# An expert layer in high and low parts: three quarters of the second weights split, one quarter plain

## The chip, the cores and the metric

One core of a Trainium2 chip runs the whole kernel. The metric is the time of one execution in microseconds (us), the median of several runs; less is better. Engines: TensorE (PE) multiplies, VectorE (DVE), ScalarE (ACT) and GpSimd (POOL) do the elementwise work, SyncE (SP) issues DMAs.

## The reference

Two layers over x, 32 sequences of 128 tokens with 256 features. The first is a cross attention with 16 heads, which is not touched here. The second sends each of the 4096 tokens to one of 8 experts, the one with the largest product with its centroid, and computes with that expert's weights

```python
xn = xhat[None, :, :] * ln_g[:, None, :] + ln_b[:, None, :]
h = jax.nn.relu(jnp.einsum('etd,efd->etf', xn, w1) + b1[:, None, :])
y = x[None, :, :] + jnp.einsum('etf,edf->etd', h, w2) + b2[:, None, :]
```

followed by a gate between y and x. Here d is 256 and f is 1024. All inputs and outputs are float32. The second product, h times w2, is what the change is about.

## The kernel before, in words

The attention stage writes each token's row, sorted by expert, to memory. The expert stage reads them back in blocks of 256 tokens of one expert. There are up to 23 blocks, and those that turn out empty are skipped at run time; blocks below n_early (6) are placed by an early table, those from 6 on by a late table that is made once all tokens are counted (late_blocks on DVE).

A float32 product on TensorE is made in one of two ways. Plain: the operands stay float32, and each product shows as two instructions. In parts: each operand is split into a high part (a copy rounded to fp32r) and a low part (the operand less its high part), and three products are summed, high with high, low with high, high with low (PASSES). Block 0 is plain altogether. From block 1 on, layer_1 (L902) is in parts, and layer_2 (layer_2_split) is in parts for the first FS of the FC = 8 chunks of the hidden width, by in_parts (L932), and plain for the other chunks, by plain (L938). Both are done for each of the two halves of 128 tokens. Before, FS is 4.

Who makes what, for block s:

- TensorE runs layer_1(s+1), then layer_2_split(s), and so on. layer_1 is made in four pairs of chunks, each into a bank of PSUM of its own, which it may write again when ReLU of the block before has read it. It waits for split_xn(s) and low_weights_1(s) as well; layer_2_split waits for all parts of the second weights and of the hidden values.
- ACT, in the order of its queue: normalise_rows(s+2) (L1186), high_weights_1(s+2) (L1170, 2048 columns), relu_parts(s+1) (L1241, four pairs), row_gain_bias(s+2) (L1208, writes c_in), high_weights_2(s+1) (L1251, the first FS chunks of w2, 256 columns each). ReLU writes the chunks that are to be split into hid_raw (y_t in the profile), the others into hid_plain (prob_t).
- DVE: low_weights_1(s+2) (L1635), split_hidden(s+1) (a cast L1644 and a subtraction L1645 for each pair of chunks), split_xn(s+2) (L1629, L1631), transpose_rows(s+3) (L1620), finish(s) (L1658 reads PSUM, L1663 writes the result rows, once for each half). Between blocks 1 and 3 it also chooses the last experts (L1509 to L1515) and makes the late table (L1561 to L1614).
- POOL: add_base(s+2) (L1891), low_weights_2(s+1) (L1898, the first FS chunks of w2), write_rows(s) (L1903, an indirect DMA for each half).
- SP loads rows, weights, vectors and biases. The first weights of blocks 6 and on are loaded once the late table is there.

Each engine works its queue in order; semaphores hold an instruction back, and what stands behind it. In split_hidden a pair of chunks is cast and subtracted, and f_hl counts it. hid_hi and hid_lo have two copies, for even and odd blocks. hid_raw has two places of 512 columns, one for each pair of a block with FS = 4.

Of the kernel before, what the change touches and what calls it, by code (L numbers as in the profile page):

```python
# [10 lines left out]
ALU = mybir.AluOpType  # L11
AXIS_X = mybir.AxisListType.X

P = 128
# [6 lines left out]
BLOCK = 2 * P  # L21
# [15 lines left out]
FIRST_SPLIT = 1  # L37
# [71 lines left out]
def build(nc, x, x_t, ctx_in, ln_pack, w_q, w_kv, w_out, w_out_t, centroids_t, consts, experts, b2, out):  # L109
# [7 lines left out]
    FC = d_ff // P  # L117
# [19 lines left out]
    with ExitStack() as top:  # L137
        def sem(name):
            return top.enter_context(nc.semaphore(name))

        def sbuf(scope, name, shape, dtype=F32):
            return scope.enter_context(nc.sbuf_tensor(name, shape, dtype))
# [23 lines left out]
        with ExitStack() as a:  # L166
# [14 lines left out]
                r_more = sbuf(late, "r_more", [P, NBLOCK - NR, 2, ROW])  # L181
            q_s = [sbuf(a, f"q_{h}", [P, 2, 2, 2 * P], F32R) for h in ("hi", "lo")]
            k_s = [sbuf(a, f"k_{h}", [P, 2, 2, BANK], F32R) for h in ("hi", "lo")]
            FS = FC // 2
            with ExitStack() as late:
                hid_hi = sbuf(late, "hid_hi", [P, 2, FS, BLOCK], F32R)
                sbuf(late, "hid_between", [P, 3 * FS * BLOCK])
                hid_lo = sbuf(late, "hid_lo", [P, 2, FS, BLOCK], F32R)
            v_n = sbuf(a, "v_n", [P, 2, 2, 2, BANK])
            y_t = sbuf(a, "y_t", [P, KC, 2, 2 * P])  # L190
            prob = sbuf(a, "prob", [P, 2, 4, 2, 2, 2, Q])
            prob_t_even = sbuf(a, "prob_t", [P, 2, 4, 2, 2, 2, Q])
# [98 lines left out]
            f_hl = sem("f_hl")  # L291
# [14 lines left out]
            def w1_raw(s):  # L306

                if s == 1:
# [9 lines left out]
            hid = v_n[:, 0].rearrange("p a b n -> p (a b n)").rearrange("p (f t) -> p f t", f=FC)  # L318
            hid_hl = (hid_hi, hid_lo)
            hid_raw = y_t[:].rearrange("p c b t -> p c (b t)")  # L320
            hid_plain = prob_t_even[:].rearrange("p b a h i s q -> p b (a h i s q)").rearrange("p s (f t) -> p s f t", f=FC - FS)
            w2_hl = [[w[:].rearrange(rule)[:, 0:FS * d_model].rearrange("p (f d) -> p f d", f=FS) for w in pair] for pair, rule in
                     ((head_out, "p b c t -> p (b c t)"), (w_o, "p c n -> p (c n)"))]
            blocks = "p (j h i s k) -> p j h i s k"
# [8 lines left out]
            raw = [w.rearrange("p (c n) -> p c n", c=KC) for w in  # L333
                   (w1_ring[:, 0], w1_ring[:, 1], r_ring[:].rearrange("p n i c -> p (n i c)")[:, 0:KC * inner])]
# [44 lines left out]
            def wait_made(eng, item):  # L379

                if item[0] == "ft":
                    eng.wait_ge(f_t, item[1] + 1)
                elif item[0] == "fy":
                    eng.wait_ge(f_y, 2 * item[1] + item[2] + 1)
                else:
                    eng.wait_ge(s_job, made_before[item] + 1)
# [70 lines left out]
            def wait_low(eng, g, side):  # L457
                if g == 0:
                    eng.wait_ge(s_lo_first[side], 1)
                else:  # L460
                    eng.wait_ge(s_lo, 2 * (g - 1) + side + 1)
# [211 lines left out]
            def _(pe):  # L673
# [245 lines left out]
                def layer_2_split(s):  # L919
# [4 lines left out]
                    def wait_parts(s):  # L924
                        pe.wait_ge(f_w2h, s - FIRST_SPLIT + 1)
                        pe.wait_ge(f_w2l, s - FIRST_SPLIT + 1)
                        pe.wait_ge(f_hl, FS // 2 * (s - FIRST_SPLIT + 1))

# [121 lines left out]
            def _(act):  # L1050
# [175 lines left out]
                def relu_parts(s):  # L1226

                    b1 = vec_ring[:, s % NR, 2 * KC:]
                    if s == FIRST_SPLIT:
                        wait_low(act, n_pairs - 1, 1)  # L1230
                        wait_made(act, ("pv", n_steps - 1))
                    for i in range(FC // 2):
                        act.wait_ge(f_h, FC // 2 * (s - 1) + i + 1)
                        if i < FS // 2 and s > FIRST_SPLIT:
                            act.wait_ge(f_hl, FS // 2 * (s - 1 - FIRST_SPLIT) + i + 1)
                        elif i == FS // 2 and s >= 2:
                            wait_made(act, ("fy", s - 2, 1))
                        for f in (2 * i, 2 * i + 1):
                            at = slice((f % 2) * BLOCK, (f % 2 + 1) * BLOCK)
                            dst = hid_raw[:, i, at] if f < FS else hid_plain[:, s % 2, f - FS, :]  # L1240
                            ins = act.activation(dst, psum[:, i, at], ACT.Relu, bias=b1[:, f:f + 1])  # L1241
                        ins.then_inc(f_ha, 1)

# [84 lines left out]
                high_outputs(n_steps - 1)  # L1328
                high_weights_1(2)
                relu_parts(1)  # L1330
                row_gain_bias(2)
                normalise_rows(3)
                high_weights_1(3)
                high_weights_2(1)
                relu_parts(2)
                row_gain_bias(3)
                gate_of(n_batches - 2)
                gate_of(n_batches - 1)
                normalise_rows(4)
                high_weights_1(4)  # L1340
                high_weights_2(2)
                relu_parts(3)
                row_gain_bias(4)
                high_weights_2(3)
# [14 lines left out]
            def _(dve):  # L1359
                chained = [0]  # L1360

                def then_next(ins):

                    chained[0] += 1
                    ins.then_inc(s_dve, 1)
                    dve.wait_ge(s_dve, chained[0])
# [271 lines left out]
                def split_hidden(s):  # L1638
                    for i in range(FS // 2):
                        dve.wait_ge(f_ha, FC // 2 * (s - 1) + i + 1)  # L1640
                        if i == 0:
                            wait_made(dve, ("fy", s - 2, 1) if s > FIRST_SPLIT else ("pv", n_steps - 1))
                        hi, lo = [h[:, s % 2, 2 * i:2 * i + 2, :].rearrange("p f t -> p (f t)") for h in hid_hl]
                        then_next(dve.tensor_copy(hi, hid_raw[:, i, :]))  # L1644
                        dve.tensor_tensor(lo, hid_raw[:, i, :], hi, ALU.subtract).then_inc(f_hl, 1)  # L1645

                def finish(s):
                    dve.wait_ge(f_b[s % NR], 16 * (s // NR + 1))
# [123 lines left out]
                places(n_batches - 3)  # L1772
                low_weights_1(2)
                split_hidden(1)
                new_rows(n_batches - 2)
                split_xn(2)
                new_rows(n_batches - 1)
                choose(n_batches - 2)
                choose(n_batches - 1)
                low_weights_1(3)  # L1780
                split_hidden(2)
                split_xn(3)
                finish(1)
                read_ranks(n_pairs - 1)
                places(n_batches - 2)
                places(n_batches - 1)
                low_weights_1(4)
                split_hidden(3)
                split_xn(4)
                late_blocks()  # L1790
# [240 lines left out]
```

## Time and profile before

| | |
|---|---|
| three runs, median | 1053.16 us (1052.61 to 1053.6) |
| the profiled execution | 1052.73 us |
| its span, first to last instruction | 1050.9 us |
| granted TensorE clock | 0.999 of full speed |
| busy: TensorE, DVE, ACT, POOL | 99%, 80%, 66%, 54% |
| DMA, mean rate | 181 GB/s |

The span is what the profile shows; its times run from the span's start. A line L938 is line 938 of the kernel. "out<-in" names tiles, and since tiles share memory, a hidden value can carry the name of an attention tile: y_t is hid_raw, prob_t is hid_plain, w_o_hi and head_out_hi are the high second weights of odd and even blocks, k_hi and k_lo the parts of the block's input, x_in the result rows.

### The profile page before, as it was taken

How to read it: one execution, taken by the hardware profiler on the slowest of the kernel's cores; microseconds unless marked ns; L12 is line 12 of the kernel's file. 1: busy time of each engine (PE TensorE's matmuls, PEld its weight loads, DVE VectorE, ACT ScalarE, POOL GpSimd, SP SyncE). 2: the span in 40 equal slices, each digit the busy share in tenths (PEclk: the TensorE clock that was granted, in tenths of full speed). 3: DMA queues.
4: the chain of work that ended last, by engine and by line, in shares of the span. 5: the costliest groups of instructions: out<-in, count | busy, mean ns of one | idle time of the engine just before them, and what ended most of it. 6: DMA issues, size and time to landing. Idle time of an engine off the chain costs nothing.

```text
span 1050.9 us, 24670 instructions
## 1 busy us (share of the span) xinstructions
PE 1041.6 (99%) x8610; PEld 940.5 (89%) x8610; DVE 844.9 (80%) x1979; ACT 688.7 (66%) x1838; POOL 565.3 (54%) x665
## 2 busy tenths in 40 slices
PE   9999999999999999999999999999999999999997
PEld 7889898988888888889898989889888999999997
DVE  7878888878888888888888879888887797767663
ACT  6765757675666767666757575766566666676761
POOL 1744464646454555545464646465444667566663
PEclk9999999999999999999999999999999999999999
DMA  6665657585757576767667585856356868777760
GB/s 212 160 169 148 170 156 189 146 215 142 201 146 197 142 193 155 200 156 197 159 168 185 142 210 137 213 144 171 91 153 196 307 198 294 250 234 234 249 194 31
DMA packets 159666, 190.57 MB, mean 181 GB/s; under 512 B 17454, under 2 KB 149038, under 8 KB 154673
## 3 DMA queue, kind: packets, MB, share of 16 engines
q1 hardware_dynamic: 155088, 179.09, 62.4%
q0 software_dynamic: 3360, 8.53, 2.2%
q8 instruction: 72, 1.18, 0.4%
q10 hardware_dynamic: 1088, 1.31, 0.4%
q14 instruction: 58, 0.47, 0.1%
HBM read 65.72 MB, written 46.07 MB: 106 GB/s over the span
## 4 chain that ended last, share of the span: by engine, by line
PE 96%; DVE 2%; POOL 1%; ACT 1%; DMA 0%; issue 0%; POOLq 0%; DVEq 0%
PE psum L742 17%; PE psum L775 16%; PE psum L812 11%; PE psum L902 10%; PE psum L791 10%; PE psum L827 9%; PE psum L761 8%; PE psum L938 6%; PE psum L932 5%; PE psum L830 1%; PE psum L883 1%; PE psum L914 1%; DVE neg_max L1410 1%; DMA c_in<-in_ctx_in 0%; PE psum L856 0%; DVE w_lo L1545 0%
## 5 line engine op out<-in xcount | busy, mean ns | idle before, releaser
L1823 POOL TENSOR_TENSOR prob<-prob,inv_sum 128x512 f32<-128x512 f32 x172 | 177.7, 1047 | 190.1 <-DVE inv_sum L1416 189.2
L1133 ACT ACTIVATE prob<-psum,neg_max 128x256 f32<-128x256 f32 x344 | 160.2, 478 | 38.8 <-DVE neg_max L1410 38.5
L1410 DVE TENSOR_REDUCE neg_max<-psum 128x2 f32<-128x512 f32 x256 | 161.9, 672 | 27.7 <-PE psum L791 27.5
L1422 DVE STREAM_TRANSPOSE prob<-prob 128x512 f32<-128x512 f32 x172 | 118.5, 698 | 12.3 <-POOL prob L1823 11.9
L1823 POOL TENSOR_TENSOR w_ring<-w_ring,inv_sum 128x512 f32<-128x512 f32 x76 | 78.1, 1041 | 76.0 <-DVE inv_sum L1416 75.7
L1140 ACT ACTIVATE head_out_hi<-psum 128x512 fp32r<-128x512 f32 x52 | 31.1, 597 | 105.6 <-PE psum L812 102.4
L1119 ACT ACTIVATE v_n<-psum 128x512 f32<-128x512 f32 x128 | 77.9, 608 | 26.7 <-PE psum L775 22.7
L1108 ACT ACTIVATE k_hi<-psum 128x512 fp32r<-128x512 f32 x128 | 77.0, 603 | 22.0 <-PE psum L742 21.3
L1461 DVE TENSOR_TENSOR k_lo<-psum,k_hi 128x512 fp32r<-128x512 f32 x128 | 85.7, 674 | 0.0
L742 PE MATMUL psum<-kv_t_hi,w_hi 128*128 128x512 f32 x252 | 85.0, 419 | 0.0
L775 PE MATMUL psum<-w_hi,kv_t_hi 128*128 128x512 f32 x256 | 80.2, 395 | 0.4 <-DVE k_lo L1461 0.4
L1133 ACT ACTIVATE w_ring<-psum,neg_max 128x256 f32<-128x256 f32 x152 | 70.7, 477 | 14.6 <-DVE neg_max L1410 14.6
L791 PE MATMUL psum<-k_hi,q_hi 64*128 64x256 f32 x512 | 79.1, 305 | 0.8 <-DVE q_lo L1468 0.7
L775 PE MATMUL psum<-w_lo,kv_t_hi 128*128 128x512 f32 x256 | 79.4, 391 | 0.0
L775 PE MATMUL psum<-w_hi,kv_t_lo 128*128 128x512 f32 x256 | 79.3, 391 | 0.0
L742 PE MATMUL psum<-kv_t_lo,w_hi 128*128 128x512 f32 x252 | 78.1, 391 | 0.0
L742 PE MATMUL psum<-kv_t_hi,w_lo 128*128 128x512 f32 x252 | 77.9, 390 | 0.0
L1133 ACT ACTIVATION_READ_ACCUMULATOR prob<-psum,neg_max 128x1 f32 x344 | 72.5, 211 | 0.0
L791 PE MATMUL psum<-k_lo,q_hi 64*128 64x256 f32 x512 | 72.5, 279 | 0.0
L791 PE MATMUL psum<-k_hi,q_lo 64*128 64x256 f32 x512 | 72.3, 278 | 0.0
L938 PE MATMUL psum<-w,prob_t 128*128 128x256 f32 x288 | 65.3, 379 | 0.0
L812 PE MATMUL psum<-w_ring,v_n 128*64 128x128 f32 x1024 | 63.0, 276 | 0.3 <-DVE cent_sum L1501 0.3
(215 smaller groups left out, 2952.4 us busy)
## 6 DMA issues: line engine op xcount, KB each, us to landing
sorted_rows<-filler SPq DMA_DIRECT2D x54, 660.0 KB
prob_t<-prob SPq DMA_DIRECT2D x172, 128.0 KB, 2.8
w_ring<-prob SPq DMA_DIRECT2D x172, 128.0 KB, 2.7
w<-in_experts SPq DMA_DIRECT2D x19, 1024.0 KB, 7.8
w_ring<-in_experts SPq DMA_DIRECT2D x18, 1024.0 KB, 6.7
prob_t<-w_ring SPq DMA_DIRECT2D x76, 128.0 KB, 2.8
w_ring<-w_ring SPq DMA_DIRECT2D x76, 128.0 KB, 2.7
w_ring<-normed SPq DMA_DIRECT2D x56, 128.0 KB, 3.0
```

Of the source, the lines that this page charges most:

```text
L742: last = pe.matmul(bank.rearrange("p (b t) -> p b t", b=2), k_w[hw][:, c, col:col + P], kv_t[hx][:, c, slot:slot + 2, :], start=(n == 0 an ...
L775: last = pe.matmul(bank, kv_t[hx][:, c, slot, side * P:(side + 1) * P], v_w[hw][:, c, col:col + BANK], start=(n == 0 and c == 0), stop=(n ...
L791: ins = pe.matmul(psum[:, 2 * bb + parity, i * 2 * P:(i + 1) * 2 * P], q_s[hq][rows, u % 2, i, bb * P:(bb + 1) * P], k_s[hk][rows, u % 2, ...
L812: last = pe.matmul(bank[rows, (2 * bb + i) * P:(2 * bb + i + 1) * P].rearrange("p (a q) -> p a q", a=4), v_n[:, h % 2, bb, side, head * DH ...
L827: pe.matmul(bank[:, 0:d_model + n_experts], heads, w_o[hw][:, c, :], start=(n == 0 and c == 0), stop=False)
L902: last = pe.matmul(dst, w1_hl[hw][s % NW][:, c, f * P:(f + 1) * P], xn_hl[hx][:, s % 2, c, :], start=(n == 0 and c == 0), stop=(n == 2 and ...
L938: last = pe.matmul(bank, hid_plain[:, s % 2, f - FS, i * P:(i + 1) * P], w2_ring[s % NW2][:, f * d_model:(f + 1) * d_model], start=(first ...
L1133: act.activation(prob_at(u, bb)[:, :, parity, i], scores_i, ACT.Exp, bias=neg_max[:, at, i:i + 1], accum_out=prob_sum[:, at, i:i + 1]).the ...
L1410: dve.tensor_reduce(neg_max[:, (4 * u + n) % 8, :], psum[:, n, :].rearrange("p (i j) -> p i j", i=2), AXIS_X, ALU.max, negate=True).then_i ...
L1422: dve.transpose(probs, probs).then_inc(s_quad, 1)
L1461: last_reads(item, dve.tensor_tensor(k_s[1][:, u % 2, i, :], work_bank(number[item]), k_s[0][:, u % 2, i, :], ALU.subtract))
L1823: pool.tensor_tensor(probs, probs, inverse, ALU.mult).then_inc(s_soft, 1)
```

## The change

FS goes from half of the chunks to three quarters, 4 to 6. So six chunks of the hidden width are split and two stay plain. The high and low second weights become 1536 columns instead of 1024, and split_hidden has three pairs instead of two. The tiles hid_hi and hid_lo grow from 4 to 6 chunks a copy; the space between them shrinks by as much, hid_lo starts where it did, and hid_plain moves to the last 1024 columns of prob_t. hid_raw keeps its two places, which are now used in turn over all pairs (0, 1, 0 in one block, 1, 0, 1 in the next). ReLU of a pair waits until the pair two before it has been split; before, it waited for the pair of the same number in the block before.

```diff
-            FS = FC // 2
+            FS = 3 * FC // 4
             with ExitStack() as late:
                 hid_hi = sbuf(late, "hid_hi", [P, 2, FS, BLOCK], F32R)
-                sbuf(late, "hid_between", [P, 3 * FS * BLOCK])
+                sbuf(late, "hid_between", [P, (2 * FC + FC // 2 - 2 * FS) * BLOCK])
                 hid_lo = sbuf(late, "hid_lo", [P, 2, FS, BLOCK], F32R)
...
-            hid_plain = prob_t_even[:].rearrange("p b a h i s q -> p b (a h i s q)").rearrange("p s (f t) -> p s f t", f=FC - FS)
+            hid_plain = prob_t_even[:].rearrange("p b a h i s q -> p (b a h i s q)")[:, FC * BLOCK - 2 * (FC - FS) * BLOCK:].rearrange(
+                "p (s f t) -> p s f t", s=2, f=FC - FS)
...
                     for i in range(FC // 2):
                         act.wait_ge(f_h, FC // 2 * (s - 1) + i + 1)
-                        if i < FS // 2 and s > FIRST_SPLIT:
-                            act.wait_ge(f_hl, FS // 2 * (s - 1 - FIRST_SPLIT) + i + 1)
+                        piece = FS // 2 * (s - FIRST_SPLIT) + i
+                        if i < FS // 2 and piece >= 2:
+                            act.wait_ge(f_hl, piece - 1)
...
-                            dst = hid_raw[:, i, at] if f < FS else hid_plain[:, s % 2, f - FS, :]
+                            dst = hid_raw[:, piece % 2, at] if f < FS else hid_plain[:, s % 2, f - FS, :]
...
-                        then_next(dve.tensor_copy(hi, hid_raw[:, i, :]))
-                        dve.tensor_tensor(lo, hid_raw[:, i, :], hi, ALU.subtract).then_inc(f_hl, 1)
+                        raw = hid_raw[:, (FS // 2 * (s - FIRST_SPLIT) + i) % 2, :]
+                        then_next(dve.tensor_copy(hi, raw))
+                        dve.tensor_tensor(lo, raw, hi, ALU.subtract).then_inc(f_hl, 1)
```

## Rows read from the trace of the kernel before

**Rows 1.** The page: busy time by engine, and the chain that ended last.

```profile
PE 1041.6 (99%) x8610; PEld 940.5 (89%) x8610; DVE 844.9 (80%) x1979; ACT 688.7 (66%) x1838; POOL 565.3 (54%) x665
...
PE 96%; DVE 2%; POOL 1%; ACT 1%; DMA 0%; issue 0%; POOLq 0%; DVEq 0%
```

**Rows 2.** The chain in order of time, expert stage: start us, us, what.

```profile
844.54 5.86 PE psum L902 x48
...
869.66 5.76 PE psum L902 x48
...
881.75 5.76 PE psum L902 x48
...
930.10 5.76 PE psum L902 x48
935.86 1.44 PE psum L932 x12
937.30 3.46 PE psum L938 x16
940.75 1.43 PE psum L932 x12
942.18 5.76 PE psum L902 x48
```

**Rows 3.** Line 938, the plain products: count, ns min/median/max, first and last start.

```profile
L938 PE MATMUL psum<-w,prob_t x288: 376/379/382, 837.5 to 1043.4; 128*128 128x256 f32 x144
```

**Rows 4.** ACT in order of time, a late block: start us, us, instruction.

```profile
936.62 1.09 ACT L1208 ACTIVATE c_in<-x_cols,vec_ring 128x256 f32<-128x256 f32 x2
937.61 1.05 ACT L1251 ACTIVATE head_out_hi<-w 128x1024 fp32r<-128x1024 f32 x1
```

**Rows 5.** ACT in order of time, blocks 2 and 6.

```profile
835.81 0.84 ACT L1241 ACTIVATE prob_t<-psum,vec_ring 128x256 f32<-128x256 f32 x2 [0.60 <-PE psum L902]
...
837.98 1.02 ACT L1208 ACTIVATE c_in<-psum,vec_ring 128x256 f32<-128x256 f32 x2
...
871.12 1.91 ACT L1170 ACTIVATE w_hi<-w_ring 128x2048 fp32r<-128x2048 f32 x1 [3.98 <-DMA w_ring<-in_experts]
```

**Rows 6.** POOL: two subtractions in order of time, and the kind of 512 columns.

```profile
834.49 2.40 POOL L1898 TENSOR_TENSOR w_o_lo<-w,w_o_hi 128x1024 fp32r<-128x1024 f32 x1
...
904.23 2.41 POOL L1898 TENSOR_TENSOR w_o_lo<-w,w_o_hi 128x1024 fp32r<-128x1024 f32 x1
...
L1816 POOL TENSOR_TENSOR kv_t_lo<-y_t,kv_t_hi 128x512 fp32r<-128x512 f32 x31 | 40.3, 1302 | 30.0 <-DVE kv_t_hi L1437 27.0 <-ACT y_t L1090 3.0
```

**Rows 7.** DVE in order of time, late blocks.

```profile
905.03 1.89 DVE L1663 SCALAR_TENSOR_TENSOR x_in<-x_in,r_more,base 128x256 f32<-128x256 f32 x1
906.85 0.41 DVE L1658 TENSOR_TENSOR x_in<-psum,x_in 128x256 f32<-128x256 f32 x1
...
907.69 2.29 DVE L1635 TENSOR_TENSOR w_lo<-w_ring,w_hi 128x2048 fp32r<-128x2048 f32 x1
909.89 0.42 DVE L1644 CAST hid_hi<-y_t 128x512 fp32r<-128x512 f32 x1
910.35 0.69 DVE L1645 TENSOR_TENSOR hid_lo<-y_t,hid_hi 128x512 fp32r<-128x512 f32 x1
...
938.20 0.69 DVE L1631 TENSOR_TENSOR k_lo<-c_in,k_hi 128x512 fp32r<-128x512 f32 x1
```

**Rows 8.** DVE in order of time, blocks 1 to 5.

```profile
834.47 2.45 DVE L1514 TENSOR_SCALAR onehot<-rank_w,rank_m 128x8 f32<-128x8 f32 x1
...
859.50 0.14 DVE L1614 CAST empty_i<-small 1x1 int32<-1x1 f32 x1
860.04 0.42 DVE L1658 TENSOR_TENSOR x_in<-psum,x_in 128x256 f32<-128x256 f32 x1 [0.41 <-issue]
...
866.66 0.92 DVE L1631 TENSOR_TENSOR k_lo<-c_in,k_hi 128x512 fp32r<-128x512 f32 x1
```

**Rows 9.** Line 1437, casts of the attention stage's input: ns min/median/max.

```profile
L1437 DVE CAST kv_t_hi<-y_t x30: 426/843/1244, 45.6 to 740.5; 128x512 fp32r<-128x512 f32 x30
```

## The prediction

> **What bounds the kernel now.** I read the page first: TensorE is busy for 99% of the span and holds 96% of the chain that ended last [rows 1]. The chain in order of time then shows the expert stage as an unbroken sequence of TensorE pieces [rows 2]: layer_1 of a block (5.76 us), split products of layer_2 (1.44), plain ones (3.46), split ones (1.43), with the next layer_1 right behind, from 930.10 so 12.08 us a block. The first blocks also carry transposes and rank products and start at 844.54, 869.66 and 881.75. There are 18 blocks with a split layer_2: its plain products give 288 instructions, 16 a block [rows 3]. So what TensorE saves is gained, as long as nothing makes it wait. The timelines of ScalarE (ACT), VectorE (DVE) and GpSimd (POOL) say how near that is.
>
> **TensorE's own part.** 12 split matmuls take 1.43 us, 0.120 each, so a product in three passes is 0.359; 16 plain instructions take 3.46, 0.216 each, two to a product, 0.432 [rows 2]. Two of four plain chunks become split, in both halves of the block: −4 × 0.432 + 12 × 0.120 = −0.29 us a block, −5.3 us over 18. A block could take 11.80 instead of 12.09. The Trainium skill (FP8 and Floating Point Precision, TensorE Precision Notes) says that true FP32 takes four passes; three equal passes would save a quarter of the plain product and the sum would be −7.8 us. The rows show only 17% saved per product, and the measured −5.3 stands.
>
> **The others' parts, each block.** The high half of the second weights goes from 1024 to 1536 columns: 1.05 us at 1024 [rows 4] and 1.91 at 2048 [rows 5] give 1.48 on ACT, +0.43. The low half on POOL takes 2.40 at 1024 and 1.30 for the same kind at 512 [rows 6]: 3.50, +1.10. DVE splits a third piece, cast and subtraction, 1.06 from start to next start (0.46 + 0.61) [rows 7]. The ReLU count is unchanged, DMAs are too; SP's queue only gets its releases later. By busy time each fits into 11.8 us. What decides is order.
>
> **The new wait.** The raw ring has two places, so ReLU pair 2 waits until DVE has split pair 0 of the same block. In DVE's queue that split stands behind finish of the block before and low_weights_1 of the block after. Behind the waiting ReLU on ACT stand ReLU pair 3, the gain and bias of the next block (which split_xn, and so TensorE's next but one layer_1, needs), the high second weights, and the row and first-weight work. So far ReLU pair 2 started as soon as TensorE had finished its products, at 835.81 in block 2 [rows 5].
>
> **The lock.** Some DVE operations on operands in SBUF do not run beside POOL's subtraction: onehot (L1514), sent at 834.47, takes 2.45 us while POOL's L1898 runs 834.49 to 836.89 [rows 6, 8]; finish's L1663, sent at 905.03, takes 1.89 and ends 0.28 after POOL's 904.23 + 2.41 [rows 6, 7]; DVE's next starts 0.21 after POOL's end. A POOL operation that is 1.10 longer delays DVE by 1.10 where they meet. Casts can wait too: the input casts take 0.43 to 1.24 us for one size, median 0.84 [rows 9]. The Trainium skill (SBUF — State Buffer, Who interferes with whom) gives the shared port pair to whoever issues first, for the whole instruction, and counts fp32 SBUF-to-SBUF casts in. By the page alone each cast that comes under the long subtraction waits with 0.45 still to go, some 1 us more over the early blocks.
>
> **The steady loop.** It closes over three engines: start of the high second weights, +1.56 to POOL's start (1.48 and a semaphore), +3.50, +0.21 to finish's second half, +0.84 to low_weights_1 (906.85 to 907.69), +2.20 to the cast (907.69 to 909.89), +0.46 + 0.69 to the end of split pair 0 [rows 7], about 0.05 to ACT, two ReLU pairs at 0.72 (an estimate from the 0.84 that one takes alone [rows 5], less what overlaps back to back), gain and bias 0.99 (936.62 to 937.61) [rows 4]: 11.94 us. This is more than TensorE's 11.80 and less than today's 12.09. So a block in the late stage gives back 0.15 instead of 0.29, once the slack of split_xn is gone (its end is at 938.20 + 0.69 now [rows 7], 3.3 us ahead of the layer_1 at 942.18). Bounds on the loop: 11.80, where TensorE rules, to 12.2 if POOL's subtraction scales to 3.60 and a cast waits.
>
> **The early blocks.** Here the slack goes at once. DVE is full: from onehot at 834.47 to the subtraction for block 5 at 866.66 + 0.92 = 867.58 [rows 8] it sits idle for 0.41 us only (before 860.04), and TensorE asks for that at 869.66, so the slack is 2.1. Added on this path: three pieces (blocks 2 to 4) 3.2, 0.2 from block 1's piece, and up to three longer lock waits, 3.3. In instants: onehot ends 1.2 later, low_weights_1 for block 3 ends about 840.7, split pair 0 about 841.9, so ReLU pair 2 starts at 842.0 instead of 835.81; the gain and bias that ran at 837.98 [rows 5] end near 844.4, split_xn(3) near 845.7, and layer_1(3), due at 844.54 − 0.29 = 844.25, waits about 1.4. The weights of block 2 come after that on ACT, near 849.1; POOL's low part ends near 852.6, or 2 later if low_weights_1 takes the lock first, and layer_2(2), due near 851.9, waits again. The tables that tell SP which experts come next end near 863 instead of at 859.64 [rows 8], hence the weights of block 6, which released ACT at 871.12 [rows 5], near 874.4, and through low_weights_1, split pair 0, ReLU 2 and 3, gain and bias, and split_xn layer_1(6) starts near 885.6 instead of 881.75. Bounds for this start: +1 (pieces only, less slack) to +7 (all lock waits, POOL last). I take +3.8: two of three lock waits make 3.5 at layer_1(5), and the late weights of block 6 add 0.3.
>
> **Sum.** +3.8 until layer_1(6); 12 blocks from there at −0.15, −1.8; the last two layer_2 (−0.6) I give away to waiting for the low weights of block 18, whose path is 1.5 longer. Together +2.0. The profiled run took 1052.73 us with a span of 1050.9, 0.43 below the median of 1053.16. The change in the span is put on the median: 1055.2.
>
> **Rivals.**
> - Nothing binds (chance 0.13). The queues settle so that ReLU waits hide, and TensorE keeps its −5.3: 1047.9. For it: busy shares of 54 to 80% on the other engines [rows 1], and 3.3 us of slack in steady blocks. Against: the early DVE queue has no room [rows 8].
> - Half the early loss (0.20). The long subtraction meets operations that need no second SBUF input; early loss about +1, then −1.8: 1052.4. For it: transposes and reads of PSUM are not held, and each delay changes which operation comes under the subtraction. Against: those of blocks 1 and 7 held one today [rows 6 to 8].
> - The loop is the longer one (0.22), the slower side. Place: POOL's low second weights holding finish, finish holding split pair 0, that holding ReLU pair 2. It decides from 0.15 us above my sum: at 12.15 each of the 12 blocks loses 0.06 instead of winning 0.15, price 2.5: 1057.7. For it: casts that wait [rows 9]. Against: TensorE's early lag would have to stay.
> - My forecast, 1053.4 to 1057: 0.45.
>
> A measurement of this kernel tells about 0.2%, 2.1 us, from no change. Faster than 1051.05: the first rival and a third of the second, 0.20. Slower than 1055.27: the third rival and 0.20 of my own case, 0.42. The rest, 0.38. The range leaves out most of the first rival and the far end of the third: 1050.2 to 1058.6.
>
> **What would show it.** L932 with 648 matmuls in place of 432, L938 with 144 in place of 288. In early blocks ReLU of pair 2 waiting for hid_lo (L1645) on ACT, 3 to 6 us; TensorE waiting at layer_1(3), (5), (6) for split_xn (L1631); L1898 at 3.5 us, L1663 up to 3 us. In the late stage layer_1 starts 11.9 apart, with a gap near 0.1 ahead of each. I am wrong if these starts are 11.80 apart without early gaps, if ReLU pair 2 starts as soon as TensorE has finished, or if they are over 12.1 apart.

## The result and the profile after

The change makes the kernel slower: 1063.34 us median (1063.23 to 1064.75, 5 runs) against 1053.47 us (1052.61 to 1053.92, 5 runs) for the kernel before on the same chip. The ratio is 1.0098, with a 95% interval of 1.0083 to 1.0113. The prediction was 1055.2 us, within 1050.2 to 1058.6. The profiled run of the change took 1064.75 us, with a span of 1062.9.

The page of the changed kernel, busy time by engine and then the engines' shares of the chain that ended last:

```profile
PE 1042.2 (98%) x8682; PEld 941.3 (89%) x8682; DVE 882.9 (83%) x2015; ACT 691.5 (65%) x1838; POOL 592.5 (56%) x665
...
PE 78%; DVE 8%; ACT 6%; issue 3%; POOL 3%; DMA 1%; SPq 0%; ACTq 0%; DVEq 0%; POOLq 0%
```

Against [rows 1], TensorE's share of the chain falls from 96 to 78%, though its busy time is about the same. The rest of the chain now runs over DVE, ACT and POOL. Where TensorE fell behind is seen in the starts of layer_1. The start of layer_1(1) is the zero point (818.34 before, 819.41 after), since the 1.07 us between these two arose ahead of the expert stage.

| | (3) | (4) | (5) | (6) | (8) | (9) | (18) | last product |
|---|---|---|---|---|---|---|---|---|
| before, us | 26.06 | 38.65 | 51.16 | 63.25 | 87.42 | 99.51 | 208.29 | 226.9 |
| after, us | 27.52 | 44.10 | 58.15 | 70.96 | 95.54 | 109.56 | 217.80 | 236.8 |
| lost | 1.5 | 5.4 | 7.0 | 7.7 | 8.1 | 10.1 | 9.5 | 9.9 |

So most is lost by layer_1(5), 2 us more between layer_1(8) and layer_1(9), and almost nothing is won in the nine blocks behind. The chain of the changed kernel in order of time, from block 2 to block 5 (start us, us, what):

```profile
850.24 5.36 POOL head_out_lo L1901
855.60 0.24 issue
855.84 3.33 PE psum L933 x18
859.17 2.35 PE psum L939 x8
861.52 2.15 PE psum L933 x18
863.67 5.76 PE psum L903 x48
...
875.89 1.66 issue
877.56 2.50 PE psum L903 x19
```

L903 is layer_1, L933 the split products (18 now, where [rows 2] have 12), L939 the plain ones (8 instead of 16), L1901 POOL's subtraction. At full clock the pieces take 2.15, 1.73, 2.15, as forecast (6.03 against 6.33). Two things are new. At 855.84 TensorE comes to layer_2(2) late, and the same pieces then take 3.33 and 2.35. At 877.56 layer_1(5) starts after 1.66 us without work.

DVE's timeline shows the second (start us, us, instruction; in brackets idle time ahead of it):

```profile
850.01 2.28 DVE L1637 TENSOR_TENSOR w_lo<-w_ring,w_hi 128x2048 fp32r<-128x2048 f32 x1
852.21 3.66 DVE L1647 CAST hid_hi<-y_t 128x512 fp32r<-128x512 f32 x1
...
861.87 4.04 DVE L1557 TENSOR_TENSOR small<-prefix,small 128x64 f32<-128x64 f32 x1
...
868.31 0.14 DVE L1616 CAST empty_i<-small 1x1 int32<-1x1 f32 x1
...
870.27 2.29 DVE L1637 TENSOR_TENSOR w_lo<-w_ring,w_hi 128x2048 fp32r<-128x2048 f32 x1
...
876.76 0.69 DVE L1633 TENSOR_TENSOR k_lo<-c_in,k_hi 128x512 fp32r<-128x512 f32 x1
```

And POOL's, for the same time:

```profile
850.24 5.35 POOL L1901 TENSOR_TENSOR head_out_lo<-w,head_out_hi 128x1536 fp32r<-128x1536 f32 x1 [7.71 <-ACT head_out_hi L1253]
...
861.26 1.08 POOL L1894 TENSOR_SCALAR base<-r_more 128x256 f32<-128x256 f32 x2
862.31 3.50 POOL L1901 TENSOR_TENSOR w_o_lo<-w,w_o_hi 128x1536 fp32r<-128x1536 f32 x1
```

DVE's last part of the input of block 5 ends at 876.76 + 0.69 = 877.45, and layer_1(5) starts 0.1 behind it. Before, that part ended at 867.58 [rows 8], 1.9 ahead of its use. Each of POOL's subtractions held one DVE instruction to its end: a cast that takes 0.42 free took 3.66, and one on 128x64 numbers that takes 0.22 took 4.04. And POOL, 0.23 behind the start of low_weights_1, took 5.35 instead of 3.50. The Trainium skill (SBUF — State Buffer, Who interferes with whom) gives a shared port pair to the first comer for its whole instruction; the held cast and POOL's wait agree, one in each direction. The instruction on 128x64 numbers goes beyond that: it was sent at 861.87, 0.44 ahead of the subtraction at 862.31, while POOL's base (861.26, 1.08) was running, and it ended only behind both. So a held instruction can wait for several POOL instructions that follow each other.

The 2 us between layer_1(8) and layer_1(9) start at the point where POOL passes from the unrolled to the conditional part of its program. POOL has no work for 5.25 us there, and its subtraction comes so late that it holds finish (POOL, then DVE):

```profile
916.06 1.09 POOL L1894 TENSOR_SCALAR base<-r_ring 128x256 f32<-128x256 f32 x2 [5.25 <-issue]
917.12 3.51 POOL L1901 TENSOR_TENSOR w_o_lo<-w,w_o_hi 128x1536 fp32r<-128x1536 f32 x1
```

```profile
917.68 3.23 DVE L1666 SCALAR_TENSOR_TENSOR x_in<-x_in,r_more,base 128x256 f32<-128x256 f32 x1
```

### The profile page after: what moved, and what is told of

It reads as the page before. It is cut to its first block, busy times and chain, and to the rows that moved or that the text cites. A ratio compares the mean times of both kernels' runs of the same rounds, so it can differ in the third digit from the quotient of the medians.

```text
span 1062.9 us, 24868 instructions
## 1 busy us (share of the span) xinstructions
PE 1042.2 (98%) x8682; PEld 941.3 (89%) x8682; DVE 882.9 (83%) x2015; ACT 691.5 (65%) x1838; POOL 592.5 (56%) x665
## 4 chain that ended last, share of the span: by engine, by line
PE 78%; DVE 8%; ACT 6%; issue 3%; POOL 3%; DMA 1%; SPq 0%; ACTq 0%; DVEq 0%; POOLq 0%
PE psum L743 17%; PE psum L776 16%; PE psum L813 11%; PE psum L792 9%; PE psum L762 8%; PE psum L828 8%; PE psum L933 2%; PE psum L903 2%; DVE w_lo L1637 2%; DVE x_in L1666 2%; ACT normed L1187 1%; DVE hid_lo L1648 1%; ACT c_in L1209 1%; PE psum L831 1%; PE psum L939 1%
## 5 line engine op out<-in xcount | busy, mean ns | idle before, releaser
L1243 ACT ACTIVATE y_t<-psum,vec_ring 128x256 f32<-128x256 f32 x108 | 43.6, 479 | 74.2 <-DVE hid_lo L1648 69.2
L903 PE MATMUL psum<-k_hi,w_hi 128*128 128x256 f32 x288 | 59.4, 288 | 5.8 <-issue 5.6
```

What stands on the lines that cost most here:

```text
L903: last = pe.matmul(dst, w1_hl[hw][s % NW][:, c, f * P:(f + 1) * P], xn_hl[hx][:, s % 2, c, :], start=(n == 0 and c == 0), stop=(n == 2 and ...
```

## The experiments

Two theories stood at first. **A**: the raw ring of two places, through ReLU's wait, makes ACT's queue and so everything behind it late. **B**: the longer subtraction on POOL does, through the port that it shares with DVE and through the low weights that come late. Runs named below as the change with an edit start from the changed kernel, the others from the kernel before.

**The ring of four places** (the change; only the raw ring differs).

```
-                        if i < FS // 2 and piece >= 2:
-                            act.wait_ge(f_hl, piece - 1)
+                        if i < FS // 2 and piece >= 4:
+                            act.wait_ge(f_hl, piece - 3)
```

> The change, but the raw ring has four places (2048 columns where the attention values lay) instead of two, so ReLU of a pair waits for the split of the pair four before, which is of the block before. Theory A (the wait of ReLU pair 2 for split pair 0 of its own block closes the loop over ACT, POOL and DVE): ReLU pairs 2 start 1.44 us apart behind TensorE again, late blocks are 11.80 us, the early loss falls under 3 us; 1047 to 1052 us. Theory B (it is the longer subtraction of POOL and the port that it shares with DVE, wherever ReLU stands): the early loss of 7 us stays, late blocks 11.8 to 12.0; 1056 to 1061 us.

Measured: ratio 1.0109 (1.0093 to 1.0126). Late blocks take 11.80, 0.23 less than in the change, but nothing is won: layer_1(3) waits 4.19 us and the block from layer_1(8) to layer_1(9) takes 18.31. TensorE's waits, and POOL's timeline at the first:

```profile
848.98 0.77 PE L902 MATMUL psum<-k_hi,w_hi 128*128 128x256 f32 x2 [4.19 <-issue]
...
923.52 1.62 PE L932 MATMUL psum<-w_o_hi,hid_hi 128*128 128x256 f32 x6 [4.85 <-POOL w_o_lo L1900]
```

```profile
844.15 3.72 POOL L1900 TENSOR_TENSOR head_out_lo<-w,head_out_hi 128x1536 fp32r<-128x1536 f32 x1 [2.22 <-ACT head_out_hi L1252]
```

Since ACT no longer waits, the subtraction starts earlier and now holds the input cast of block 3 (844.51, 3.64 us). A alone is not the cause. The time, 1064.81 us, also lies above what B had (1056 to 1061). Of the 6.2 us too much at layer_1(9), 4.85 are the wait, and most of the rest is the lower granted clock that follows it (see the last section).

**The wait alone** (before, with a wait of ReLU pair 2 for the split of pair 0).

```
+                        if i == FS // 2:
+                            act.wait_ge(f_hl, FS // 2 * (s - FIRST_SPLIT) + 1)
```

> The kernel before with one wait more: ReLU pair 2 (a plain one here) waits until split pair 0 of its block is done. No work is added. Theory A: the early blocks lose 1 to 4 us, since gain and bias, first and second weights of the next blocks all come later; late blocks stay at 12.09, since the loop with a subtraction of 2.40 us is 10.4; 1055 to 1058 us. Theory B: no change, 1053 to 1054 us.

Measured: 1.0050 (1.0033 to 1.0067). Late blocks stay at 12.09; layer_1(5) is 3.5 us later. DVE sits idle 1.57 us for the gain and bias (ACT) in each of blocks 3, 4 and 5.

**The long subtraction alone** (before, with 1536 columns subtracted, of which 512 are not used).

```
-                    pool.tensor_tensor(w2_hl[s % 2][1], raw, w2_hl[s % 2][0], ALU.subtract).then_inc(f_w2l, 1)
+                    hi, lo = [w[:].rearrange(rule)[:, 0:6 * d_model] for w in pair]
+                    pool.tensor_tensor(lo, w2_ring[s % NW2][:, 0:6 * d_model], hi, ALU.subtract).then_inc(f_w2l, 1)
```

> The kernel before, but POOL subtracts 1536 columns of the second weights instead of 1024; the 512 more are not used by anything. Theory A: little, 1053 to 1055 us, since ReLU and with it the next block's inputs are tied to nothing. Theory B: longer lock waits of VectorE in the full early blocks cost most of what the change costs, 1057 to 1060 us; late blocks stay at 12.09.

Measured: 1.0046 (1.0029 to 1.0063). Three blocks are longer and no other: the one that ends at layer_1(3), 16.03 us, the next, 13.93, and the one from layer_1(8) to layer_1(9), 16.03. So either theory's part alone costs about 5 us in a kernel that has none of TensorE's gain, A's ahead of layer_1(5) and (6), B's ahead of layer_1(3), (4) and (9), and neither costs anything in the steady blocks.

**The change with the short subtraction** (1024 columns; the low part of a third of the split second weights is left out of the result).

> The change, but POOL makes the low part of the second weights for four chunks only, so chunks 4 and 5 are multiplied with what lies in that tile: this leaves out a third of the low second weights. The subtraction is 2.40 us again. Theory A: ReLU pair 2 still waits, the early loss stays at 3 us or more, the loop is 10.8 and late blocks 11.80; 1051 to 1056 us. Theory B: the early loss is gone; 1047 to 1050 us.

Measured: 1.0010 (1.0001 to 1.0020), late blocks 11.80 or 11.86. The median is 0.8 us above that of before, so of the change's 9.9 us the length of POOL's instruction is worth some 9. But theory B's forecast did not come true: layer_1(5) is still 3.8 us late, and the time is the one that A had. The remaining +0.8 is the balance of what TensorE saves, some 5, and of what the ring, DVE's third piece and the holds that stay still cost, some 6. The parts do not simply add up.

**Where the second loss arises** (the change, low weights of block 7 ahead of the point where POOL passes from its unrolled to its conditional part).

```
+                low_weights_2(n_early + 1)
                 empty = count_empty(pool)
```

> The change, with one step of POOL moved: the low weights of block 7 are subtracted in the unrolled part, ahead of the reading of empty_i and of the drain between the two parts, so that they no longer wait behind POOL's 5.25 us without work at 910.8. Theory (the hand-over of POOL makes TensorE late once, when the subtraction is long): the block of 14.02 us before layer_1(9) shrinks to 12.0 to 12.6 and the run to 1061.5 to 1062 us, ratio 1.0080 to 1.0085. Rival (those 5 us are only moved, and the subtraction for block 8 is late in its place, or TensorE's lag at that point was absorbed anyway): 1.0095 to 1.0100 as the change.

Measured: 1.0107 (1.0092 to 1.0122), the rival's side. Block 8 to 9 takes 12.04, but 9 to 10 takes 14.29 and 10 to 11 takes 13.37. The idle time came back as a late base (923.23, behind 3.88 us without work); the base and the subtraction of the next block follow, and that subtraction holds DVE's finish (POOL, then DVE):

```profile
929.07 1.09 POOL L1894 TENSOR_SCALAR base<-r_ring 128x256 f32<-128x256 f32 x2
930.13 3.50 POOL L1901 TENSOR_TENSOR head_out_lo<-w,head_out_hi 128x1536 fp32r<-128x1536 f32 x1
```

```profile
930.43 3.49 DVE L1666 SCALAR_TENSOR_TENSOR x_in<-x_in,r_ring,base 128x256 f32<-128x256 f32 x1
```

**Three edits together** (the change, with the ring of four places, the move just shown, and the edit that follows).

> The change with three things together: raw ring of four places, the low weights of block 7 ahead of the hand-over, and POOL's subtraction in two instructions (1024 and 512 columns) for which TensorE waits only in the third pass, where it first reads them. Theory (everything the change loses is lost at these places): late blocks 11.80, no long block 8, and only the early DVE cast held by POOL's port (4.19 us before layer_1(3) in the ring-of-four run) stays; 1053.5 us, ratio 1.000, between 0.997 and 1.003. Rival (the losses are POOL's load as such, and come up elsewhere): 1.006 or more.

Measured: 1.0046 (1.0030 to 1.0062), between the two sides. From layer_1(7) on all blocks take 11.80; before it TensorE waits 4.13 at layer_1(3) and 3.87 at layer_1(6). Single runs lie between 1054.48 and 1061.05, so this order is not the same each time.

**TensorE waits later for the low weights** (the change).

```
+                    for part in (slice(0, 4), slice(4, FS)):
+                        pool.tensor_tensor(w2_hl[s % 2][1][:, part], ...).then_inc(f_w2l, 1)
...
+                                if waits and hw == 1 and f in (0, 4):
+                                    pe.wait_ge(f_w2l, 2 * (s - FIRST_SPLIT) + (1 if f == 0 else 2))
```

> The change, with POOL's subtraction in two instructions of 1024 and 512 columns, each with its own count, and TensorE waits for each where it first reads it, in the third pass, instead of before the first. Theory (2.48 us of waiting for the low weights of block 2, then a lower granted clock that costs 1.8 more): that wait shrinks to under 0.5, the granted clock stays at full, and block 4 is 2 to 4 us shorter; block 8's wait for the same operand shrinks as well by 1 to 2; the run 1058 to 1060.5 us, ratio 1.0045 to 1.0070. Rival (the wait was not what made the later ones, which are the ring's and DVE's): 1.009 to 1.010.

Measured: 1.0105 (1.0090 to 1.0119): the theory fell. The wait at layer_2(2) did shrink, to 0.67, and layer_1(4) came 3.5 us earlier. All of it was given back one block on, behind a DVE instruction that is held by POOL's base and by both parts of the subtraction, 4.76 us instead of 0.17 (TensorE, then DVE):

```profile
876.44 0.77 PE L903 MATMUL psum<-k_hi,w_hi 128*128 128x256 f32 x2 [5.16 <-DVE k_lo L1634]
```

```profile
859.78 4.76 DVE L1608 SCALAR_TENSOR_TENSOR small<-small,taken 128x8 f32<-128x8 f32 x1
```

layer_1(5) stands 58.19 behind layer_1(1), as in the change (58.15). So the wait at 855.84, with the clock that fell behind it, cost nothing of its own at layer_1(5). The edit has a price too: the two parts of the subtraction take 3.66 us together, and late blocks take 12.17. This gave **theory C**: up to layer_1(5) DVE's queue sets the time, and ring, third piece and port all act through it.

**Six chunks only from block 8 on** (four up to block 7; ring of four places throughout).

```
+            S6 = n_early + 2
+            def split_chunks(s):
+                return FS if s >= S6 else FC // 2
```

> Four chunks in parts up to block 7, as before, and six from block 8 on, with a raw ring of four places throughout. Theory (the change gains 0.29 us in every steady block when the ring lets it, and loses only where attention's rest and the hand-over of POOL meet the longer steps): blocks up to 8 as before, from there 11.80 each, 10 to 11 blocks, so 2.9 to 3.2 us gained less up to 0.7 in the tail: 1050.5 to 1051.5 us, ratio 0.9973 to 0.998. Rival (the switch to six starts a loss of its own, as any start of longer POOL work): ratio 1.000 or more.

Measured: 1051.28 us, ratio 0.9981 (0.9972 to 0.9989), as expected. Up to layer_1(9) every start is that of before to 0.3 us, then each block takes 11.80. The chain of this kernel in order of time, at the passage:

```profile
918.23 5.76 PE psum L919 x48
923.99 2.16 PE psum L949 x18
926.15 1.73 PE psum L955 x8
927.88 2.15 PE psum L949 x18
930.03 5.76 PE psum L919 x48
```

**DVE's third piece alone** (before, pair 1 split twice).

```
+                        if i == 1:
+                            then_next(dve.tensor_copy(hi, hid_raw[:, i, :]))
+                            then_next(dve.tensor_tensor(lo, hid_raw[:, i, :], hi, ALU.subtract))
```

> The kernel before, in which DVE splits the second pair of every block twice (0.41 and 0.69 us more a block, the same values), and nothing else is changed. Theory (in blocks 2 to 5 DVE has no free time: between 834 and 872 it is idle once, 0.41 us, so layer_1(5) starts when DVE's queue lets it): three more pieces before the last part of the input of block 5 are 3.3 us, less 0.4 idle and the 1.9 us between that part (867.6) and layer_1(5) (869.50), so layer_1(5) 1.0 us later and nothing more after block 6: 1054.0 us, ratio 1.001; up to 1.003 if the shifted instructions meet POOL's subtraction more often. Rival (DVE's load is hidden, and the wait for the ring and for POOL's result alone cost the time): 1.000 within 0.0005.

Measured: 1.0057 (1.0044 to 1.0070), far more than my 1.001. layer_1(5) starts at 875.06, 4.7 us later relative to layer_1(1), and again 0.1 behind DVE's last part. The three extra pieces are 3.3 us, as counted. But they shift DVE's casts under POOL's subtraction, which is as short as before, and one more meeting falls ahead of layer_1(5): DVE is held four times there, 8.9 us in all, where it was held three times before, 5.9 us:

```profile
855.65 3.06 DVE L1629 CAST k_hi<-c_in 128x512 fp32r<-128x512 f32 x1
...
871.21 3.02 DVE L1629 CAST k_hi<-c_in 128x512 fp32r<-128x512 f32 x1
874.26 0.69 DVE L1631 TENSOR_TENSOR k_lo<-c_in,k_hi 128x512 fp32r<-128x512 f32 x1
```

Each should take 0.43. The rival, that DVE's load is hidden, is out.

**Six chunks from block 6, and from block 4** (as above, S6 = 6 and 4).

> As the kernel with six chunks from block 8 on, but from block 6 on. Theory of DVE's queue (it is full only up to block 5, from there it has 2.5 us and more free in each block): two more blocks gain 0.29 us each, layer_1(5) unmoved at 51.2 us behind layer_1(1), ratio 0.9975 against 0.9981. Rival (the hand-over of POOL before the subtraction of block 7 bites as soon as that subtraction is long): one block of 13 to 14 us between layer_1(7) and layer_1(9), ratio 0.9985 to 1.000.

> The same with six chunks from block 4 on. Theory of DVE's queue: the third piece of block 4 and one longer hold of the port come ahead of the last part of the input of block 5, 1.1 to 2.2 us against 1.9 us of slack, so layer_1(5) is 0 to 0.4 us later and the other blocks gain 0.29 each: ratio 0.997 to 0.998. Rival (six chunks in any block before the steady part start the waits for the ring and for POOL): 1.000 to 1.004.

Measured: 0.9989 (0.9978 to 1.0000) and 1.0015 (1.0004 to 1.0026). layer_1(5) is unmoved in both, 51.16 us behind layer_1(1), as theory C has it. But in the profiled runs the block from layer_1(8) to layer_1(9) takes 15.34 and 17.73 us, more than the rival's 13 to 14, and both ratios lie where the rivals had them. TensorE and POOL with six from block 6:

```profile
913.34 0.95 PE L949 MATMUL psum<-w_o_hi,hid_hi 128*128 128x256 f32 x6 [1.76 <-POOL w_o_lo L1920]
```

```profile
905.91 3.55 POOL L1912 TENSOR_SCALAR base<-r_ring 128x256 f32<-128x256 f32 x2 [6.31 <-issue]
909.44 3.65 POOL L1920 TENSOR_TENSOR w_o_lo<-w,w_o_hi 128x1536 fp32r<-128x1536 f32 x1
```

POOL has no work for 6.31 us at its passage, then base (3.55, where the change's took 1.09), then the long subtraction, and layer_2(7) is due before that. The base is long since DVE's low_weights_1 (906.92, 2.28) holds it. Of the 3.5 us too much, 1.76 are TensorE's wait; the other 1.8 are the lower granted clock behind it, with which the pieces of layer_2 take 3.35, 2.33 and 2.16 us.

**The tables behind the input of block 5** (the change; 8 us of DVE work moved back).

```
-                late_blocks()
+                read_totals(("total",))
                 finish(2)
...
+                    if s == 3:
+                        late_blocks()
```

> The change, with the tables of the late blocks made behind the input of block 5 on DVE instead of ahead of the low weights of block 5, which takes 8.0 us (860.47 to 868.45, 3.8 of them held by POOL) from ahead of layer_1(5). Theory of DVE's queue: layer_1(5) starts 51 to 53 us behind layer_1(1) instead of 58.15. SyncE can load the rows and weights of block 6 only when the tables are made, some 6 to 7 us later than in the change, so layer_1(6) comes at 70 to 73 us behind layer_1(1), as in the change (70.96), and the run ends within 2 us of it: 1.008 to 1.011. Rival (the wait of 2.48 us for POOL and the fall of the clock made layer_1(5) late, not DVE): layer_1(5) at 57 us or more.

Measured: 1.0209 (1.0196 to 1.0223). layer_1(5) comes at 56.06, between the two sides (2.1 us earlier than in the change, not 5 to 7): DVE's last part is ready at 54.6, since finish came under POOL in the place of the tables (4.88 us instead of 0.48), and TensorE itself, with its early wait, comes later still. The price of late tables I had badly low: the loads of block 6 start only when the tables are there (880.5), and layer_1(6) waits 13.95 us.

**The move ahead of the passage, without the early loss** (six chunks from block 6, and from block 4, each with low weights 7 moved as above).

> Six chunks from block 6 on, with the low weights of block 7 subtracted ahead of POOL's hand-over (its reading of empty_i, the drain and the first conditional step). Theory (the hand-over leaves POOL idle 6.3 us, and the 3.65 us of the subtraction and the 3.55 us of the base behind it are what the 15.34-us block waited for): no block over 12.1 us, 1050.0 us, ratio 0.9970 to 0.9978. Rival (the idle time comes behind the subtraction and makes that of block 8 late, as the move did in the change): a block of 13 to 15 us between layer_1(8) and layer_1(10), ratio 0.9985 or more.

> Six chunks from block 4 on, with the same move ahead of the hand-over. Theory of DVE's queue and of the hand-over together: layer_1(5) unmoved (in the run without the move it stood 51.16 us behind layer_1(1), as before), the block of 17.73 us gone, 14 blocks of 11.80: ratio 0.9965 to 0.9975. Rival: as for the kernel beside it, 0.9985 or more.

Measured: 1050.76 us, ratio 0.9975 (0.9965 to 0.9984), and 1.0000 (0.9989 to 1.0010). With six from block 6 the long block is gone (11.80) and one of 13.52 stands ahead of layer_1(6), where the theory had none over 12.1. This ratio is the lowest of the study, but its interval overlaps those of six from block 8 (0.9981) and of six from block 6 without the move (0.9989), so what the move is worth is not shown. With six from block 4 the loss is spread, 14.81 and 13.35 us ahead of layer_1(8) and (9), and the rival's side came true.

All starts of layer_1 that decide, from the profiled runs:

| kernel | ratio | last input part of block 5 ready | layer_1(5) | layer_1(8) to (9) | late block |
|---|---|---|---|---|---|
| before | 1 | 49.2 | 51.16 | 12.09 | 12.09 |
| the change | 1.0098 | 58.0 | 58.15 | 14.02 | 12.03 |
| ring of four | 1.0109 | 57.4 | 57.45 | 18.31 | 11.80 |
| wait alone | 1.0050 | 54.6 | 54.67 | 12.09 | 12.09 |
| long subtraction alone | 1.0046 | 54.2 | 55.34 | 16.03 | 12.09 |
| short subtraction | 1.0010 | 54.9 | 55.00 | 11.89 | 11.80 |
| later wait | 1.0105 | 58.1 | 58.19 | 12.61 | 12.17 |
| third piece alone | 1.0057 | 55.8 | 55.90 | 12.31 | 12.09 |
| six from 8 | 0.9981 | 49.2 | 51.16 | 12.09 | 11.80 |
| six from 6, moved | 0.9975 | 50.1 | 51.16 | 11.80 | 11.80 |

(Columns 3 and 4 in us behind layer_1(1).) Nine kernels start layer_1(5) 0.1 us behind DVE's last part: in the table the change, the ring of four, the wait alone, the short subtraction, the later wait and the third piece alone, and besides these the change with the move (58.13), the three edits together (57.15) and six from 4 with the move (51.43).

A trace is one execution, and where meetings decide, executions differ. Single runs of six from 6 lie between 1049.74 and 1056.42 us (median 1051.53, the profiled one 1053.89), those of six from 4 between 1051.51 and 1056.97, so the long block need not be in each of them; those of six from 8 lie within 0.75 us. Six from 6 and the same with the move also have the same code up to POOL's subtraction of block 7, and yet layer_1(6) stands 63.25 us behind layer_1(1) in the one trace and 64.68 in the other: there POOL held a DVE instruction of the tables for 2.74 us from 854.56 on, where in the other it held a later one for 1.92, and the tables, the weights of block 6 and the input of block 6 came later.

## Why the prediction was wrong

- **TensorE's own part held.** −0.29 us a block: where nothing waits a block takes 11.80, as computed, and 12.09 before. (Over 18 blocks that is −5.2; the prediction has −5.3.)
- **The new wait held.** ReLU pair 2 of block 2 waited 6.63 us for DVE and started at 843.16, 842.1 less the later start of the stage, where 842.0 was forecast; layer_1(3) waited 0.85 instead of 1.4. ACT's waits for DVE's splits add up to 69 us over the kernel:

```profile
L1243 ACT ACTIVATE y_t<-psum,vec_ring 128x256 f32<-128x256 f32 x108 | 43.6, 479 | 74.2 <-DVE hid_lo L1648 69.2
```

- **The step that failed: "I take +3.8: two of three lock waits make 3.5 at layer_1(5)."** Measured: +7.0 at layer_1(5) and +7.7 at layer_1(6), above even my bound of +7 for that start. The path was the right one, DVE's queue up to the last part of the input of block 5, and so was the slack (1.9 measured, 2.1 taken). The term that was too small is the lock's: 2.2 us taken, two holds that are 1.1 longer each; measured 4.3, three holds that are longer by 1.0 (835.78), 1.3 (852.21) and 2.1 (861.87). From the start of low_weights_1(3) to that of low_weights_1(5) DVE needed 24.64 us before (837.19 to 861.83) and 31.03 after (839.24 to 870.27). Of the 6.4 more, two third pieces are 2.1, as priced; the two holds there grew from 3.7 to 7.1, so 3.4; waits for ACT, which the prediction put at nothing, are 0.4; the other 0.5 are small delays of single instructions. I had priced a hold by the growth of the subtraction, as if the same instructions met at the same instants. But when all is shifted, other instructions meet. A meeting can cost the whole of what POOL still has to do, and not only the growth of it. The run with the third piece alone shows this with the short subtraction: 4.7 us where the pieces less slack make 1.
- **What was missing: POOL's passage to its conditional part**, which the kernel before has as well (4.62 us idle ahead of 903.18) and hides. With a longer subtraction it is uncovered: +1.9 between layer_1(8) and (9), and up to 6 in the experiments, of which up to 1.8 are the granted clock's. The prediction has no term for it. POOL's timeline of before has it just ahead of the second row of [rows 6]:

```profile
903.18 1.09 POOL L1891 TENSOR_SCALAR base<-r_ring 128x256 f32<-128x256 f32 x2 [4.62 <-issue]
```

- **The steady loop: 11.94 forecast, 12.03 measured.** That it binds between TensorE's 11.80 and 12.09 was right, and so was its path. In the change (ACT, POOL, then DVE):

```profile
927.56 1.49 ACT L1253 ACTIVATE head_out_hi<-w 128x1536 fp32r<-128x1536 f32 x1
```

```profile
929.13 3.53 POOL L1901 TENSOR_TENSOR head_out_lo<-w,head_out_hi 128x1536 fp32r<-128x1536 f32 x1 [1.27 <-ACT head_out_hi L1253]
```

```profile
931.69 1.25 DVE L1666 SCALAR_TENSOR_TENSOR x_in<-x_in,r_ring,base 128x256 f32<-128x256 f32 x1
932.87 0.41 DVE L1661 TENSOR_TENSOR x_in<-psum,x_in 128x256 f32<-128x256 f32 x1
933.31 0.48 DVE L1666 SCALAR_TENSOR_TENSOR x_in<-x_in,r_ring,base 128x256 f32<-128x256 f32 x1
933.72 2.28 DVE L1637 TENSOR_TENSOR w_lo<-w_ring,w_hi 128x2048 fp32r<-128x2048 f32 x1
```

From the high weights to POOL 1.57, POOL 3.53, to finish's second half 0.21, to low_weights_1 0.85, and so on to the next high weights at 939.59: each step within 0.05 us of the forecast. The chain of the profile goes over ACT's normalising of the rows and DVE's transposition instead, since it takes the 1.25 us for DVE's own work; finish takes 0.49 where nothing holds it and ends 0.28 behind POOL here. The nine blocks from layer_1(9) to (18) won 0.5 us against before instead of 1.4. The loop needs both parts, ring and subtraction: 11.80 with either one cured, 12.09 in the kernels where either was added alone. Nor is it fixed by the code: with the change's own late part, but another start (the move in the change), blocks took 11.80 from layer_1(11) to layer_1(17). Why the loop did not bind there stays open.
- **The tail**: I gave away what the last two layer_2 save, 0.6; the table of starts shows another 0.4 lost. With it the 7.9 us between +2.0 and +9.9 are: 3.9 up to layer_1(6), 2.8 from there to layer_1(9), 0.8 in the nine blocks behind, 0.4 in the tail.
- **The rivals.** The half early loss and the one in which nothing binds are refuted by the rows above. The longer loop named the right pair, port and ring, but put the loss in the steady blocks, where there was none.

## What to carry to other kernels

When a queue without free time shares a lock with another engine, price added work there not by its own length but by the meetings that it can shift: each can cost the whole length of the other's instruction, or of several in a row. Removing one wait on such a queue moved the loss and did not lower it, three times here; what helped was to leave the full stretch as it was and to make the change only where the queue has room. Look for one-time passages of a program (from unrolled to conditional code) and ask what covers them.

## What the hardware showed beyond that

TensorE's granted clock fell after the early wait. The windows of the changed kernel (window in us, then busy time of PE, PEld, DVE, ACT and POOL; PEclk is the column behind POOL's):

```profile
852.80:855.80 3.00, 0.56 (x6) 0.32 (x3) 3.00 (x1) 0.00 (x0) 2.83 (x2) 1.00 0.00 0
855.80:857.80 2.00, 1.96 (x13) 1.99 (x14) 1.93 (x5) 1.11 (x4) 1.70 (x2) 0.77 0.18 66
857.80:859.20 1.40, 1.40 (x8) 1.40 (x8) 1.04 (x3) 1.40 (x5) 1.09 (x2) 0.50 0.01 0
859.20:861.50 2.30, 2.30 (x10) 1.91 (x10) 2.12 (x7) 2.30 (x4) 1.95 (x3) 0.76 0.33 119
861.50:863.50 2.00, 2.00 (x19) 2.00 (x18) 1.97 (x2) 1.82 (x2) 2.00 (x3) 1.00 0.19 68
```

TensorE had worked 0.56 of the 3.0 us up to its return; within 2 us behind it the clock went from 2.4 GHz to 1.2 (0.50) for some microseconds, and the pieces of 2.15 and 1.73 took 3.33 and 2.35, 1.8 us more. The same fall follows waits of 1.76 us (six from 6), 2.70 (long subtraction alone), 3.04 (wait alone), 3.23 (the move in the change) and 5.16 (later wait), and none follows the 1.04 us ahead of layer_2(2) in the move. But the length of the wait is not the whole of it: the clock stayed whole behind the 1.66 and 1.82 us ahead of layer_1(5) and (9) in the change and behind 2.33 ahead of layer_1(5) with the short subtraction, and behind 2.77 us ahead of layer_1(5), with DVE's third piece alone, too:

```profile
872.30:875.00 2.70, 0.00 (x0) 0.00 (x0) 2.67 (x3) 0.00 (x0) 1.64 (x1) 1.00 0.96 378
875.00:877.00 2.00, 1.94 (x16) 1.97 (x17) 1.86 (x5) 0.96 (x1) 0.33 (x1) 1.00 0.77 324
```

A wait of TensorE can thus have a second price. In the change it was hidden by the later wait for DVE; with six from 6 it is half of the long block. What decides whether the clock falls stays open here.

POOL's passage from unrolled to conditional code left it without work for 4.47 to 7.52 us, depending on the kernel, and for 3.9 where the subtraction was moved ahead of it. What it does there (reading a register from memory, a drain, a branch) was not taken apart and stays open.
